# Local attention in 64-query blocks and couples of pairs, with probabilities normalised on GpSimd

## The reference

```
qkv = shift(x) @ Wqkv                         # half the columns one token late; 16 heads of 64
q, k = rotary(l2norm(q)), rotary(l2norm(k))
sim  = 8 * q @ k.T                            # a query sees itself and the 32 keys before it
attn = softmax(where(mask, -big, sim))
x   += (attn @ v) @ Wo
x   += (a * gelu(gate)) @ W2 + b2             # a, gate = layernorm(shift(x)) @ W1 + b1, 341 each
```

## Time and profile before

| | |
|---|---|
| median of 3 runs | 6041.95 us (6040.45 to 6043.06) |
| the profiled execution | 6046.58 us, span 6044.8 us |
| granted TensorE clock, mean | 0.949 |
| TensorE busy | 5374.6 us, 89% |
| VectorE busy | 4235.2 us, 70% |
| ScalarE busy | 3913.8 us, 65% |
| GpSimd busy | 2701.1 us, 45% |

### The profile page before, as it was taken

How to read it: one execution, slowest core, us unless ns; L and a number is a source line. 1 busy time by engine, 2 the same in 40 slices (tenths; PEclk the granted TensorE clock), 3 DMA queues, 4 the chain that set the end, 5 groups by cost and what they waited for, 6 DMA issues and landing times. The chain is left out here.

```text
span 6044.8 us, 121573 instructions
## 1 busy us (share of the span) xinstructions
PE 5374.6 (89%) x41154; PEld 3795.8 (63%) x41154; DVE 4235.2 (70%) x16128; ACT 3913.8 (65%) x11510; POOL 2701.1 (45%) x2580
## 2 busy tenths in 40 slices
PE   7885799999999999997499999999999999697989
PEld 5674466666666666665256666666666666464678
DVE  4453788888888888885488888888888887454522
ACT  2211588888888888884178888888888888222333
POOL 0000556566565665652166566565565655230000
PEclk9996899999999999998599999999999999697999
DMA  0000000000000000000000000000000000000000
GB/s 11 22 1 3 22 1 12 9 12 9 5 12 6 12 9 12 8 1 4 21 1 11 8 3 12 9 12 9 7 10 6 12 8 1 5 2 4 2 29 8
DMA packets 30964, 53.45 MB, mean 9 GB/s; under 512 B 7688, under 2 KB 17168, under 8 KB 29712
## 3 DMA queue, kind: packets, MB, share of 16 engines
q1 hardware_dynamic: 30352, 45.66, 2.4%
HBM read 44.60 MB, written 1.05 MB: 8 GB/s over the span
## 5 line engine op out<-in xcount | busy, mean ns | idle before, releaser
L1791 PE MATMUL bank<-wA,next_rowT 128*128 128x512 f32 x2304 | 1217.0, 630 | 206.7 <-DVE turnB L2141 88.6
L1995 ACT ACTIVATE pairs<-pairs,negmax 128x128 f32<-128x128 f32 (+1 forms) x3072 | 1236.9, 418 | 8.0 <-DVE negmax L2102 7.0
L1972 POOL TENSOR_TENSOR turnA<-raw,ropes 128x512 f32<-128x512 f32 x768 | 969.1, 1272 | 152.6 <-ACT raw L2019 123.8
L2102 DVE CUSTOM_DVE_ANT_0 pairs<-bank,bands,big 128x128 f32<-128x128 f32 (+1 forms) x3072 | 940.6, 362 | 62.9 <-PE bank L1720 59.4
L1979 POOL TENSOR_TENSOR qk<-turnA,turnB 128x512 f32<-128x512 f32 x768 | 976.4, 1272 | 6.4 <-DVE turnB L2141 6.4
L1951 POOL COPY spread<-recip 128x256 f32<-128x256 f32 x768 | 305.6, 398 | 1262.7 <-DVE recip L2111 1256.9
L1791 PEld LDWEIGHTS bank<-wA,next_rowT 128*128 128x128 f32 x2304 | 370.8, 191 | 689.1 <-DVE turnB L2141 286.3
L2002 ACT ACTIVATE pairsT<-bank 128x512 f32<-128x512 f32 x768 | 465.9, 607 | 303.7 <-PE bank L1733 303.4
L1995 ACT ACTIVATION_READ_ACCUMULATOR pairs<-pairs,negmax 128x1 f32 x3072 | 624.7, 203 | 0.0
L285 POOL TENSOR_TENSOR rstd<-vareps,neg_half 128x2 f32<-128x2 f32 x56 | 39.0, 696 | 1288.4 <-DVE vareps L256 892.3
L2141 DVE TENSOR_TENSOR turnB<-bank,ropes 128x512 f32<-128x512 f32 x768 | 522.4, 680 | 0.0
(11 more groups left out here) (313 smaller groups left out, 11261.8 us busy)
## 6 DMA issues: line engine op xcount, KB each, us to landing
wA<-in_wt_wqkv SPq DMA_DIRECT2D x72, 256.0 KB, 2.8
wB<-in_wt_wo SPq DMA_DIRECT2D x12, 512.0 KB, 3.5
wC<-in_wt_w SPq DMA_DIRECT2D x12, 341.0 KB, 2.9
wD<-in_wt_w SPq DMA_DIRECT2D x12, 192.0 KB, 2.3
big<-in_e_up SPq DMA_DIRECT2D x1, 2048.0 KB
big<-in_e_down SPq DMA_DIRECT2D x1, 2048.0 KB
scl<-in_wt_scales SPq DMA_DIRECT2D x12, 128.0 KB, 3.3
X<-in_x SPq DMA_DIRECT2D x8, 128.0 KB, 2.3
```

The costliest lines, as they stand in the source:

```text
L1791: pe.matmul(side_bank(i)[:, :], c.next_rowT[:, t * P:(t + 1) * P], wqkv[:, k * 512:(k + 1) * 512], start=True, stop=True).then_inc(s.chunk ...
L1972: g.tensor_tensor(c.turnA[:, m % 2, :].rearrange("p (h d) -> p h d", h=8), c.raw[:, m % 4, :].rearrange("p (h d) -> p h d", h=8), cos, ALU ...
L1995: last = a.activation(tile, tile, ACT.Exp, scale=-1.0, bias=c.negmax[:, 2 * p + side, t:t + 1], accum_out=c.pair_sums[:, p % 4, t, side:si ...
L2102: last = v.tensor_tensor_reduce(c.pairs[:, 2 * (p % 4) + side, AT[t]:AT[t] + SPAN[t]], c.bank[side][:, AT[t]:AT[t] + SPAN[t]], c.bands[:, ...
```

## The change

- **Blocks.** The scores are computed for 64 queries by 96 keys (`BLOCK`, `BLOCK_KEYS`), the first block of a sequence by 64 keys, on quarters of TensorE's array. A tile of 128 partitions holds two blocks, so the minima, exponentials and masks work on tiles of 128 by 96, four a pair. The mask is an input now, loaded in the setup, not built by GpSimd.
- **Couples.** Scores, weighing and the copy of the context are done for two pairs at once, so four times a turn.
- **Shares.** GpSimd multiplies the probabilities by the reciprocals (`pool_shares`) before TensorE turns them. `pool_spread`, the turning of the shares, their copy and `dve_share` go. So does `dve_turn_prev`.
- **Values.** The values of each 96-key block are laid out on partitions 0 to 95 by six DMAs a turn from SP's queue (`sp_values`); V has one buffer, and its copies wait for the layout of the turn before. SP's queue is written by turns.
- **Context.** `pe_weigh` writes the turned context of a couple to one bank, and ScalarE copies it (`act_copy_ctx`).
- **Order.** In a slot, TensorE turns the next pair's probabilities at the end; scores come at the start of even slots, weighing at the end of odd slots; the gates stand ahead of the scores in slot 6. The first roots move from slot 2 to slot 3, behind the copy of the late keys and the statistics.

Of the functions that set the order (`pe_window`, `act_window`, `dve_window`) the new lines stand alone here.

```diff
-DVE_RSQRT_SLOTS = {2: 0, 6: 1}
+DVE_RSQRT_SLOTS = {3: 0, 6: 1}
...
-        def pe_scores(pe, T, p):
+        def pe_scores(pe, T, n):
             j = T % 2
-            if p % 2 == 0:
-                pe.wait_ge(s.qT_copied, T * 4 + p // 2 + 1)
-                pe.wait_ge(s.kT_copied, T * 4 + p // 2 + 1)
-            if T * PAIRS + p > T0 * PAIRS:
-                pe.wait_ge(s.negmax_ready, T * PAIRS + p)
-            for t in range(HALVES):
-                for side in range(2):
-                    q, k = [x[j][DH * side:DH * side + DH, p, :] for x in (qT, kT)]
-                    last = pe.matmul(c.bank[side][:, AT[t]:AT[t] + SPAN[t]], q[:, t * P:(t + 1) * P],
-                                     k[:, FIRST_KEY[t]:FIRST_KEY[t] + SPAN[t]], start=True, stop=True,
-                                     skip_group_check=True)
+            pe.wait_ge(s.qT_copied, T * 4 + n + 1)
+            pe.wait_ge(s.kT_copied, T * 4 + n + 1)
+            if T > T0 or n > 0:
+                pe.wait_ge(s.negmax_ready, T * PAIRS + 2 * n)
+            for e in range(2):
+                for t in range(HALVES):
+                    for w in range(2):
+                        q0 = t * P + w * BLOCK
+                        k0 = max(q0 - WINDOW, 0)
+                        keys = q0 + BLOCK - k0
+                        at = (2 * e + t + 1) * BLOCK_KEYS - keys
+                        for side in range(2):
+                            q, k = [x[j][DH * side:DH * side + DH, 2 * n + e, :] for x in (qT, kT)]
+                            last = pe.matmul(c.bank[side][w * BLOCK:(w + 1) * BLOCK, at:at + keys], q[:, q0:q0 + BLOCK],
+                                             k[:, k0:k0 + keys], start=True, stop=True, skip_group_check=True)
             last.then_inc(s.scores_ready, 1)
         def pe_turn_probs(pe, T, p):
-            pe.wait_ge(s.probs_ready, T * PAIRS + p + 1)
-            if T * PAIRS + p > T0 * PAIRS:
-                pe.wait_ge(s.probsT_ready, T * PAIRS + p)
-            for side in range(2):
-                probs, out = c.pairs[:, 2 * (p % 4) + side, :], c.bank[2][:, S * side:S * side + S]
-                pe.transpose(out[:, 0:P], probs[:, 0:P], c.ident[:, :])
-                last = pe.transpose(out[:, P:2 * P], probs[:, P + WINDOW:2 * P + WINDOW], c.ident[:, :])
+            pe.wait_ge(s.shares_ready, T * PAIRS + p + 1)
+            if T * PAIRS + p - 1 > T0 * PAIRS:
+                pe.wait_ge(s.probsT_ready, T * PAIRS + p - 1)
+            for g in range(4):
+                last = pe.transpose(probs_bank(p)[0:BLOCK_KEYS, g * P:(g + 1) * P], pairs[:, p % 4, g, :], c.ident[:, :])
             last.then_inc(s.probsT_in_psum, 1)
-        def pe_shares(pe, T, p):
-            pe.wait_ge(s.spread_ready, T * PAIRS + p + 1)
-            if T * PAIRS + p - 1 > T0 * PAIRS:
-                pe.wait_ge(s.ctx_ready, T * PAIRS + p - 1)
-            for t in range(HALVES):
-                pe.transpose(c.bank[4 + p % 2][:, S + t * P:S + (t + 1) * P], c.spread[:, p % 2, t * P:(t + 1) * P],
-                             c.ident[:, :])
-        def pe_weigh(pe, T, p):
-            pe.wait_ge(s.probsT_ready, T * PAIRS + p + 1)
-            pe.wait_ge(s.prev_ready, T * PAIRS + p + 1)
-            if p == 0:
-                pe.wait_ge(s.chunk_copied, (T + 1) * N_CHUNKS)
-            out = c.bank[4 + p % 2]
-            for kt, q0, q1 in ((0, 0, P + WINDOW), (1, P, S)):
-                at = 0 if kt == 0 else P + WINDOW
-                for side in range(2):
-                    last = pe.matmul(out[DH * side:DH * side + DH, q0:q1], V[T % 2][:, kt, 2 * p + side, :],
-                                     c.pairsT[:, 2 * (p % 2) + side, at:at + q1 - q0], start=(kt == 0), stop=(kt == 1),
-                                     skip_group_check=True)
+        def pe_weigh(pe, T, n):
+            pe.wait_ge(s.probsT_ready, T * PAIRS + 2 * n + 2)
+            pe.wait_ge(values_laid[n // 2], VALUE_PARTS * (T + 1))
+            if T > T0 or n > 0:
+                pe.wait_ge(s.ctx_ready, T * COUPLES + n)
+            for e in range(2):
+                for t in range(HALVES):
+                    for w in range(2):
+                        at = t * P + w * BLOCK
+                        for side in range(2):
+                            turned = c.probsT[0:BLOCK_KEYS, e, 2 * side * P + at:2 * side * P + at + BLOCK]
+                            last = pe.matmul(c.bank[4][DH * side:DH * side + DH, e * S + at:e * S + at + BLOCK],
+                                             values[n // 2][0:BLOCK_KEYS, 2 * t + w, 4 * (n % 2) + 2 * e + side, :], turned,
+                                             start=True, stop=True, skip_group_check=True)
             last.then_inc(s.ctx_in_psum, 1)
...
         def pe_window(pe, T):
             following = has_turn(T + 1)
+            for slot in range(PAIRS):
+                n = slot // 2
+                if slot % 2 == 0:
+                    if slot == 0 and following:
+                        pe_xT(pe, T + 1)
+                    if slot == 6 and has_turn(T - 2):
+                        pe_gates(pe, T - 2, (s.qT_copied, (T + 1) * 4 + (1 if following else 0)))
+                    if n + 1 < COUPLES:
+                        pe_scores(pe, T, n + 1)
+                    elif following:
+                        pe_scores(pe, T + 1, 0)
+                for i in PE_LATE_QKT_SLOTS.get(slot, ()):
                     pe_turn_qk(pe, T, i)
+                if slot == 1 and has_turn(T - 3):
                     pe_ff_out(pe, T - 3)
+                if slot == 2 and has_turn(T - 2):
                     pe_shift(pe, T - 2)
+                if slot == 6 and has_turn(T - 1):
                     pe_out(pe, T - 1, (s.kT_copied, (T + 1) * 4 + (1 if following else 0)))
+                if slot == 7 and has_turn(T - 2):
                     pe_linear(pe, T - 2)
                 if following:
+                    pe_prepare(pe, T + 1, slot, False)
+                if slot == 5 and has_turn(T - 2):
                     pe_turn_normed(pe, T - 2)
+                if slot % 2 == 1:
+                    pe_weigh(pe, T, n)
+                if slot + 1 < PAIRS:
+                    pe_turn_probs(pe, T, slot + 1)
+                elif following:
+                    pe_turn_probs(pe, T + 1, 0)
...
-        def pool_spread(g, T, p):
+        def pool_shares(g, T, p):
             g.wait_ge(s.recip_ready, T * PAIRS + p + 1)
-            if T * PAIRS + p - 2 >= T0 * PAIRS:
-                g.wait_ge(s.ctx_in_psum, T * PAIRS + p - 1)
-            g.tensor_copy(c.spread[:, p % 2, :].rearrange("p (n d) -> p n d", n=4),
-                          c.recip[:, 0, 4 * (p % 4):4 * (p % 4) + 4].unsqueeze(2).broadcast_to((P, 4, DH))
-                          ).then_inc(s.spread_ready, 1)
+            shares = c.recip[:, 0, 4 * (p % 4):4 * (p % 4) + 4].unsqueeze(2).broadcast_to((P, 4, BLOCK_KEYS))
+            g.tensor_tensor(pairs[:, p % 4, :, :], pairs[:, p % 4, :, :], shares, ALU.mult).then_inc(s.shares_ready, 1)
...
-        def act_copy_shares(a, T, p):
-            a.wait_ge(s.ctx_in_psum, T * PAIRS + p + 1)
-            a.activation(c.shares[:, p % 2, :], c.bank[4 + p % 2][:, S:2 * S], ACT.Identity).then_inc(s.shares_ready, 1)
+            a.activation(c.probsT[0:BLOCK_KEYS, p % 2, :], probs_bank(p)[0:BLOCK_KEYS, :], ACT.Identity).then_inc(s.probsT_ready, 1)
+        def act_copy_ctx(a, T, n):
+            a.wait_ge(s.ctx_in_psum, T * COUPLES + n + 1)
+            a.activation(part_of(ctxT[T % 2], n), c.bank[4][:, :], ACT.Identity).then_inc(s.ctx_ready, 1)
...
-                h0 = 8 * (k - QK_CHUNKS)
-                last = a.activation(V[q % 2][:, t, h0:h0 + 8, :], src.rearrange("p (h d) -> p h d", h=8), ACT.Identity)
+                part, h0 = k - QK_CHUNKS, 8 * (k - QK_CHUNKS)
+                if q > 0:
+                    a.wait_ge(values_laid[part], VALUE_PARTS * q)
+                last = a.activation(V[:, t, h0:h0 + 8, :], src.rearrange("p (h d) -> p h d", h=8), ACT.Identity)
...
         def act_window(a, T):
             following = has_turn(T + 1)
+            for slot in range(PAIRS):
+                n = slot // 2
                 if following:
+                    for i in ACT_CHUNK_SLOTS.get(slot, ()):
                         act_copy_chunk(a, T + 1, i)
+                    if slot == 6:
                         act_copy_q(a, T + 1, 0)
+                act_copy_probs(a, T, slot)
+                if slot % 2 == 0:
+                    if slot == 0 and following:
+                        act_xT(a, T + 1)
+                    if n >= 1:
+                        act_copy_ctx(a, T, n - 1)
+                    elif has_turn(T - 1):
+                        act_copy_ctx(a, T - 1, COUPLES - 1)
+                    if slot == 6 and has_turn(T - 2):
+                        act_normedT(a, T - 2)
+                    if slot == 0:
+                        act_copy_q(a, T, COPY_LATE_QKT_SLOTS[slot])
```

(91 more changed lines are left out.)

223 lines of the change are left out of this document (68 added, 155 removed).

## The result

The changed kernel takes 6272.97 us (median of 4 runs, 6262.7 to 6275.43) against 6041.61 us: a ratio of 1.038, 95% interval 1.0362 to 1.0398. That is slower by 231 us; 6,200 was forecast, 158 us above before.

A forecast was written before the change was run, and what follows sets the result against it. TensorE seemed the limit, but with TensorE, VectorE and ScalarE moving in step, order was expected to decide: 6,042 us plus 100 for order and 60 for clock falls gave 6,200, range 6,080 to 6,350.

The forecast's parts named there:

- The walk: Instructions of all engines placed through one new turn: 45.5 us, 1.1 more than now; 6,080 to 6,350 us total, chance 0.66.
- The pauses: TensorE's waits in one turn of the changed kernel: 1.4, 3.0, 1.8 and twice 0.7 us.
- The chain copy, statistics, roots, rotations, minima: VectorE's work in a row from slot 3's keys copy at 15.5: 7.8 us, to 23.3, with TensorE waiting for the first rotation.
- the pause of slot 5: TensorE waits three us before chunk 10, as ScalarE squares the new chunks only after pair 6's exponentials, which wait for minima.
- The order's term: Loss from instruction order: 1.1 us a turn over some 92 turns, +100 us.
- The clock's term: TensorE's clock falls to half after pauses: one fall in every second turn, 0.65 us a turn, +60 us.
- Slot 7's pause: TensorE's turning of the keys waits for GpSimd's scaling, which follows VectorE's second roots and ends at 43.4 us.
- The prices: Durations given to each engine's instructions, such as 0.82 us for a couple's scores, 1.05 its weighing, 0.9 GpSimd's product.
- The sum: TensorE's work added up without waits: 44.4 us a turn less the savings, 38.8.
- (b): Rival: TensorE's sum decides, 38.8 us a turn giving 5,525 us, or 5,840 with half the walk's loss; chance 0.25.
- (c): Rival: matmuls run two abreast, or 64 columns cost as much as 128; 6,350 to 6,600 us, chance 0.05.
- (d): Rival: all effects cancel, the turn stays 44.4 us, time within 0.2%; chance 0.04.

The follow-up runs named there:

- one_newton: Changed kernel with two of the three Newton steps of the roots left out (inverse norms less exact): 6064.6 us, ratio to before 1.0039.
- stats_warm: Changed kernel with filling matmuls in slots 5 and 6 and slot 3's statistics ahead of the late keys' copy: 6078.9 us, ratio to before 1.0059.
- rotate_first: On top of both: chunks 8 and 9 copied before pair 6's exponentials, value copies and slot 5's rotations moved ahead, no fillers: 5697.6 us, ratio to before 0.9431.
- warm: Changed kernel, order kept, with unread identity turnings filling TensorE's pauses, 24 in slot 5 and 14 in slot 6: 6152.1 us, ratio to before 1.0185.
- gates_last: Changed kernel with slot 6 reordered: gates behind scores and output, gelu behind the exponentials: 6031.9 us, ratio to before 0.9981.
- stats_look: Changed kernel with slot 3's statistics ahead of the late keys' copy, no fillers, run again for its profile: 6257.9 us in one execution.
- both: Changed kernel with slot 6's gates behind scores and output, and statistics ahead of the late keys' copy, no fillers: 6004.9 us, ratio to before 0.9938.
- both_warm: The kernel of both plus 24 filling matmuls in slot 5 alone: 5898.7 us, ratio to before 0.9761.

## Why the prediction was right

**The walk held, point by point.** Times from the end of the turning of pair 0, forecast and measured (timeline above, less 1230.92): slot 3's copy of the keys 15.5 and 15.9; chunk 10 26.8 and 27.1; gates 33.9 and 34.3; end of the second roots 41.4 and 42.1; the turn 45.5 and 45.8. The pauses were put at 1.4, 3.0, 1.8 and twice 0.7; they are 1.07, 2.76, 1.62, and in slot 7 0.86 and in slot 0 0.34 and 0.39. The chain copy, statistics, roots, rotations, minima was forecast to the instruction: one_newton and stats_warm show that what is taken from it comes off the turn. The reason given for the pause of slot 5, ScalarE's squares behind pair 6's exponentials, is confirmed by rotate_first, where the pause falls to 0.58.

**The order's term** was +1.1 a turn, 100 us; measured, it is 45.8 - 44.6 = 1.2 a turn, and 110 us by warm.

**The clock's term was mis-sized**: one fall in every second turn, 0.65 a turn, 60 us. By warm it is 121 us, 1.3 a turn. The price of a fall was right (121 us by 92 stretches, 1.3 each); there is about one a turn, not one in two. Of the 92 stretches at 0.50, 71 begin 26 to 29 us into the turn, behind the pause of slot 5, and 21 at 35 to 36.5, behind the gates'; in gates_last, where the second pause is gone, all 49 begin at 26 to 29. Counting each of the two pauses as a possible fall would have been nearer. Why the fall comes in some turns and not in others stays open.

**One releaser was wrong.** Slot 7's pause was put on GpSimd's scaling of the keys, 43.4. The view of waits names VectorE's product of the hidden rows, L2190, which stands behind the roots. The scaling of that slot is for the other half of the heads, and it was still running when TensorE began to turn at 1274.00:

```profile
1273.14 1.91 POOL L1970 TENSOR_TENSOR qk<-qk,big 128x1024 f32<-128x1024 f32 x1 [7.61 <-DVE recip L2221]
```

That this step still gave nearly the right time is luck: the product and the scaling both come right behind the same roots.

**The prices.** Scores 0.82 (0.82 forecast), weighing 1.08 (1.05), the statistic 0.17 (0.2), a pair's minima 0.95 (0.93; the forecast's lower bound, in proportion to columns, should have been 1.15 x 384 / 576 = 0.77, not 0.86). GpSimd's product is in the groups of the changed kernel (count, then busy us and mean ns of one), forecast at 0.9:

```profile
L1938 POOL TENSOR_TENSOR pairs<-pairs,recip 128x384 f32<-128x384 f32 x768 | 634.4, 826 | 470.1 <-DVE recip L2097 467.6
```

The TensorEngine Tiling page of the Trainium skill (Performance Considerations, Instruction Overhead) would, by the estimate made before, have a couple at 1.0 and 1.45; the trace disagrees, with 0.82 and 1.08.

**The sum was near by luck.** The pauses of the turn shown are 0.34, 0.39, 0.24, 1.07, 2.76, 0.29, 1.62 and 0.86, together 7.6 us. Windows over that turn and over one of before (columns as in the earlier trace rows):

```profile
1230.92:1276.72 45.80, 38.01 (x414) 25.87 (x415) 29.43 (x130) 35.15 (x109) 29.91 (x26) 1.00 0.13 33
```

```profile
1476.41:1521.04 44.63, 42.30 (x303) 29.42 (x304) 36.52 (x147) 36.86 (x115) 26.72 (x28) 1.00 0.03 8
```

TensorE's work fell from 42.3 to 38.0 us a turn, by 4.3, where the prices gave 5.6. The forecast took the whole 44.4 us for TensorE's work, though 2.3 us of a turn were pauses. The two errors nearly cancel, so the sum's 38.8 lies near 38.0. Some of what the prices missed shows in the timeline: a turning behind a weighing takes 0.57 (1249.99 to 1250.56), not 0.44. VectorE's work is 29.4, where 29 was forecast.

**The rivals.** (b), TensorE's sum, did not decide in this order, but it is nearer to what the blocks are worth: with the order mended the turn is 40.8, 2.8 us above TensorE's own 38.0. Its place was put at slot 4 alone; the runs needed slot 6 (gates_last, 2.0 us a turn), slot 3 with 4 (stats_warm, 0.8) and slot 5 (rotate_first, 2.2). (c) and (d) fall by the prices and the result.

## What to carry to other kernels

A sum of work says what a change can be worth, a walk through the order says what it will be: here the two differed by 7 us a turn, and 5 us came back by moving instructions that were already there. When a change takes work off the busiest engine, look at the waits that its work had hidden; a step put ahead of the scores because it fits there (the gates) holds up everyone who lives on them. And a pause costs twice where the clock falls behind it: read the undisturbed turn and the half-clock time apart, since a repair of the order (the statistics) can be real and still not show in the total.

## What the runs showed of the hardware beyond that

The half-clock time does not follow the sum of the pauses. stats_look has less pause a turn than the changed kernel (0.8 less) and 451 us at 0.50 against 317; gates_last has 184 with the same 2.76 us pause in slot 5, and both, with slot 4's pause gone as well, 283. What a us at half clock costs on the path varies less. By runs with and without fillers it is 121 / 317 = 0.38 for the changed kernel against warm, 106 / 283 = 0.37 for both against both_warm, and 187 / 451 = 0.41 for the statistics (6266.3 and 6078.9). By the 88 turns against undisturbed ones, as an estimate, it is 65 / 184 = 0.35 in gates_last and 133 / 416 = 0.32 in one_newton.

VectorE's scalar operation on two columns (L2180, L2205 before) lasts 0.17 us in all 96 turns of the changed kernel, where no GpSimd instruction runs beside it. Before, it lasted 1.25 us at the median, ending with an addition on GpSimd, and 0.17 in the six turns that had none beside it.
